# A two-layer attention and expert kernel: layer 0's projections in the order q, k, relative positions of two lines each, V, with a bank of its own for V

## What is computed

```python
qkv = x @ w_qkv + b_qkv                          # q, k, v: (12 heads, 256, 16)
rel_h = jnp.einsum('bhwc,hkc->bhwk', qr, Rh)     # qr = q as (12, 16, 16, 16)
rel_w = jnp.einsum('bhwc,wkc->bhwk', qr, Rw)
attn = jnp.einsum('bmd,bnd->bmn', q, k) * scale
attn = attn + rel_h[:, :, :, :, None] + rel_w[:, :, :, None, :]
p = jax.nn.softmax(attn, axis=-1)
o = jnp.einsum('bmn,bnd->bmd', p, v)
return o @ w_o + b_o
```

## Time and profile before

| | us |
|---|---|
| median of 3 runs | 238.82 |
| lowest, highest | 236.95, 240.77 |
| the profiled execution | 235.63 |
| its span, first to last instruction | 233.6 |
| TensorE busy in it | 216.7 |
| mean granted TensorE clock | 0.957 of full |

### The profile page before, as it was taken

The page is one execution under the profiler, slowest core; times in us unless marked ns, Lnnn a source line. Parts: engine busy times, 40 slices in busy tenths (PEclk is TensorE's granted clock), DMA queues, the critical chain, the costliest instruction groups (busy, mean ns, idle before and its releaser), DMA issues.

```text
span 233.6 us, 4218 instructions
## 1 busy us (share of the span) xinstructions
PE 216.7 (93%) x1580; PEld 195.1 (84%) x1580; DVE 103.6 (44%) x334; ACT 68.5 (29%) x197; POOL 37.0 (16%) x60
## 2 busy tenths in 40 slices
PE   7999989869999999999999989799869999999992
PEld 7799877549898999999999789575558999999991
DVE  2340687568623122222222234886569564723221
ACT  2031087525221212222222131666522021211100
POOL 5220300011990000000000014000014950000000
PEclk9996799997999999999999999958999999999997
DMA  6999999936000000000000000999900000500001
GB/s 169 349 425 423 438 454 424 440 140 153 0 3 0 3 0 0 3 1 0 3 0 0 3 6 15 369 425 426 385 6 1 0 0 15 191 0 3 0 3 41
DMA packets 4492, 31.05 MB, mean 133 GB/s; under 512 B 584, under 2 KB 2064, under 8 KB 2192
## 3 DMA queue, kind: packets, MB, share of 16 engines
q1 hardware_dynamic: 4464, 30.69, 33.6%
HBM read 30.50 MB, written 0.20 MB: 131 GB/s over the span
## 4 chain that ended last, share of the span: by engine, by line
PE 90%; ACT 4%; issue 2%; DVE 2%; POOL 0%; DVEq 0%; ACTq 0%; POOLq 0%
PE bank L1150 17%; PE bank L1137 13%; PE bank L916 9%; PE bank L1135 8%; PE bank L1139 7%; PE bank L985 6%; PE bank L1158 5%; PE bank L940 5%; PE bank L1036 4%; PE bank L970 4%; PE bank L997 3%; PE bank L1122 3%; PE bank L1167 1%; ACT scratch L517 1%; DVE neg_max L661 1%
## 5 line engine op out<-in xcount | busy, mean ns | idle before, releaser
L1150 PE MATMUL bank<-w,scratch 128*96 128x192 f32 (+2 forms) x228 | 52.0, 330 | 0.1
L1137 PE MATMUL bank<-xe_lo,w 128*128 128x192 f32 (+3 forms) x168 | 43.3, 339 | 0.0
L750 DVE TENSOR_TENSOR scratch<-scratch,bank 128x96 f32<-128x96 f32 (+5 forms) x60 | 15.2, 253 | 52.8 <-ACT scratch L475 52.8
L1150 PEld LDWEIGHTS bank<-w,scratch 128*96 128x96 f32 (+2 forms) x228 | 30.7, 164 | 1.5 <-issue 0.3
L475 ACT ACTIVATE scratch<-bank 128x96 f32<-128x96 f32 (+5 forms) x60 | 15.0, 249 | 55.3 <-PE bank L1139 55.3
L1135 PE MATMUL bank<-scratch,w 128*128 128x96 f32 (+3 forms) x168 | 30.8, 265 | 0.0
L1135 PEld LDWEIGHTS bank<-scratch,w 128*128 128x128 f32 (+3 forms) x168 | 27.7, 185 | 3.0 <-issue 3.0
L1139 PE MATMUL bank<-scratch,w 128*128 128x96 f32 (+3 forms) x168 | 29.9, 259 | 0.0
L1139 PEld LDWEIGHTS bank<-scratch,w 128*128 128x128 f32 (+3 forms) x168 | 29.0, 185 | 0.4
L517 ACT ACTIVATE scratch<-bank,neg_max 128x256 f32<-128x256 f32 x48 | 19.8, 477 | 18.9 <-DVE neg_max L661 18.9
L1137 PEld LDWEIGHTS bank<-xe_lo,w 128*128 128x128 f32 (+3 forms) x168 | 24.9, 187 | 0.0
(11 more groups left out here) (160 smaller groups left out, 254.4 us busy)
## 6 DMA issues: line engine op xcount, KB each, us to landing
w<-experts_dram SPq DMA_DIRECT2D x9, 1152.0 KB, 12.3
w<-experts_dram SPq DMA_DIRECT2D x1, 3624.0 KB, 41.8
w<-experts_dram SPq DMA_DIRECT2D x1, 3024.0 KB, 33.7
w<-experts_dram SPq DMA_DIRECT2D x1, 2496.0 KB, 26.6
w<-experts_dram SPq DMA_DIRECT2D x1, 2016.0 KB, 21.2
w<-experts_dram SPq DMA_DIRECT2D x1, 1704.0 KB, 16.9
w<-experts_dram SPq DMA_DIRECT2D x1, 1416.0 KB, 12.2
w<-experts_dram SPq DMA_DIRECT2D x1, 1272.0 KB, 9.3
```

Of the source, the lines that this page charges most:

```text
L750: nc.vector.tensor_tensor(hidden[0:m, n % RING, 0], silu_g[0:m, n % 2, :], up_bank(n)[0:m, 1], ALU.mult).then_inc(sems["hidden_vec"], 1)
L1137: nc.tensor.matmul(tile.rearrange("p u s -> p (u s)"), w0[:, begin + short:begin + short + m], lo.rearrange("p u s -> p (u s)"), start=Fal ...
L1150: ins = nc.tensor.matmul(y_bank(e)[0:SLOTS, 0:C], hidden[0:m, n % RING, u], w0[0:m, begin + at:begin + at + C], start=t == 0 and u == 0, s ...
```

## The change

In layer 0 the order becomes q, k, relative positions, V; in layer 1 it stays k, q, V. V goes to bank 6 in both layers. Each relative-position product takes two lines (96 columns); the second line's result is wrong for that window, and the next product writes over it. The last line of an axis is taken alone. `rel_psum` counts up after each half of an axis, so ScalarE and VectorE start on a half as soon as it is there, and VectorE goes by halves first and groups second. V waits for ScalarE's copies of the first axis, which read bank 6. V's bias is added after the maximum of head 2, in both layers, and the wait for it moves from the first turn to the first weighing. The products on `ones` before the scores of layer 0 go from 10 to 2, and 4 more (`KEEP_FIRST`) are put between the second pair of scores and the first turn, in both layers. q's weights are loaded ahead of k's, and `rel_t` ahead of V's and the parameters. The routing is the same in both kernels.

```diff
-KEEP_START, KEEP_SCORES, KEEP_ROUTE, KEEP_PLACE, KEEP_NORM = 12, (10, 7), 6, 5, 16
+KEEP_START, KEEP_SCORES, KEEP_FIRST, KEEP_ROUTE, KEEP_PLACE, KEEP_NORM = 12, (2, 7), 4, 6, 5, 16
...
+            sp.dma_start(att[0:CH, :, W_Q:W_K], weights[0][:, :, W_Q:W_K]).then_inc(q_landed, 16)
             sp.dma_start(att[0:CH, :, W_K:W_V], weights[0][:, :, W_K:W_V]).then_inc(k_landed, 16)
-            sp.dma_start(att[0:CH, :, W_Q:W_K], weights[0][:, :, W_Q:W_K]).then_inc(q_landed, 16)
+            sp.dma_start(rel_t[:], rel_in).then_inc(rel_landed, 16)
             sp.dma_start(att[0:CH, :, W_V:W_END], weights[0][:, :, W_V:W_END]).then_inc(rest_landed, 16)
             sp.dma_start(par[:], params).then_inc(par_landed, 16)
-            sp.dma_start(rel_t[:], rel_in).then_inc(rel_landed, 16)
...
-                            pool.wait_ge(rel_ready, 2 * (g + 1))
+                            pool.wait_ge(rel_ready, HG + g + 1)
...
-                    act.wait_ge(rel_psum, 1)
                     for half in range(2):
+                        act.wait_ge(rel_psum, half + 1)
...
+                def add_v():
+                    dve.wait_ge(v_psum, layer + 1)
+                    dve.wait_ge(par_landed, 16)
+                    for t in range(TT):
+                        nc.vector.tensor_tensor(v1[:, t, :, 0:HD], bank[6][:, t * C:(t + 1) * C].rearrange("p (h d) -> p h d", d=HD),
+                                                par[:, layer, B_V:B_V + C].rearrange("p (h d) -> p h d", d=HD), ALU.add).then_inc(v_ready, 1)
...
-                    dve.wait_ge(rel_psum, 2)
                     dve.wait_ge(rel_half, 2)
-                    for g in range(HG):
-                        for half, b in enumerate((7, 3)):
+                    for half, b in enumerate((7, 3)):
+                        dve.wait_ge(rel_psum, 3 + half)
+                        for g in range(HG):
...
-                        dve.wait_ge(rel_ready, 2 * (g + 1))
-                        nc.vector.tensor_copy(rel_hi[:, g], relT[:, g]).then_inc(rel_rounded, 1)
+                            if half == 1:
+                                dve.wait_ge(rel_ready, HG + g + 1)
+                                nc.vector.tensor_copy(rel_hi[:, g], relT[:, g]).then_inc(rel_rounded, 1)
...
+                    if h == 2:
+                        add_v()
...
+                if g == 0:
+                    pe.wait_ge(v_ready, TT * (layer + 1))
...
+                    project_q()
+                    pe.wait_ge(k_landed, 16)
+                    project_k()
...
-                            last = nc.tensor.matmul(bank[banks[i // 8]][:, at:at + HG * GRID], window, lines[:, i],
+                            wide = 1 if i + 1 == GRID else 2
+                            last = nc.tensor.matmul(bank[banks[i // 8]][:, at:at + wide * HG * GRID], window, lines[:, i:i + wide],
                                                     start=True, stop=True)
-                        last.then_inc(rel_psum, 1)
+                            if i % 8 == 7:
+                                last.then_inc(rel_psum, 1)
+                    pe.wait_ge(rest_landed, 16)
+                    pe.wait_ge(rel_half, 2)
+                else:
+                    project_k()
+                    project_q()
+                for t in range(TT):
+                    last = project_tokens(bank[6][:, t * C:(t + 1) * C], t, slice(W_V, W_V + C))
+                last.then_inc(v_psum, 1)
...
                 scores(layer, 1)
-                pe.wait_ge(v_ready, TT * (layer + 1))
+                keep_clock(KEEP_FIRST, 5)
```

More of the change, by code:

```diff
@@ L640, in attend @@
                                                    ALU.mult, ALU.add).then_inc(q_split, 1)
-                    if g == 0:
-                        dve.wait_ge(v_psum, layer + 1)
-                        dve.wait_ge(par_landed, 16)
-                        for t in range(TT):
-                            nc.vector.tensor_tensor(v1[:, t, :, 0:HD], bank[4][:, t * C:(t + 1) * C].rearrange("p (h d) -> p h d", d=HD),
-                                                    par[:, layer, B_V:B_V + C].rearrange("p (h d) -> p h d", d=HD), ALU.add).then_inc(v_ready, 1)
                 if layer == 0:
-                    dve.wait_ge(rel_psum, 2)
                     dve.wait_ge(rel_half, 2)
-                    for g in range(HG):
-                        for half, b in enumerate((7, 3)):
+                    for half, b in enumerate((7, 3)):
+                        dve.wait_ge(rel_psum, 3 + half)
+                        for g in range(HG):
                             cols = relT[:, g, :].rearrange("p (r c) -> p c r", c=GRID)[:, 8 * half:8 * half + 8]
@@ L1003, in attend, with project_k, project_q @@
             def attend(layer):
-                if layer == 0:
-                    pe.wait_ge(k_landed, 16)
-                else:
+                if layer == 1:
                     pe.wait_ge(att_landed, 16)
-                for g in range(HG):
-                    last = project(bank[g // 2][:, (g % 2) * TOK:(g % 2 + 1) * TOK],
-                                   W_K + g * P)
-                last.then_inc(k_psum, 1)
+                def project_k():
+                    for g in range(HG):
+                        last = project(bank[g // 2][:, (g % 2) * TOK:(g % 2 + 1) * TOK], W_K + g * P)
+                    last.then_inc(k_psum, 1)
+                def project_q():
+                    for g in range(HG):
+                        last = project(bank[2 + g // 2][:, (g % 2) * TOK:(g % 2 + 1) * TOK], W_Q + g * P)
+                    last.then_inc(q_psum, 1)
                 if layer == 0:
                     pe.wait_ge(q_landed, 16)
-                for g in range(HG):
-                    last = project(bank[2 + g // 2][:, (g % 2) * TOK:(g % 2 + 1) * TOK], W_Q + g * P)
-                last.then_inc(q_psum, 1)
-                if layer == 0:
-                    pe.wait_ge(rest_landed, 16)
-                for t in range(TT):
-                    last = project_tokens(bank[4][:, t * C:(t + 1) * C], t, slice(W_V, W_V + C))
-                last.then_inc(v_psum, 1)
-                if layer == 0:
+                    project_q()
+                    pe.wait_ge(k_landed, 16)
+                    project_k()
                     pe.wait_ge(rel_landed, 32)
```

## The result

| | us |
|---|---|
| changed kernel, median of 4 runs (lowest, highest) | 230.44 (228.84, 231.82) |
| kernel before, median of its 4 runs beside them | 239.45 (236.95, 240.77) |
| ratio, with its 95% interval | 0.9655 (0.9544 to 0.9766) |
| profiled execution: time, span | 230.48, 228.4 |
| mean granted clock in it | 0.982 (before 0.957) |

The change makes the kernel faster by 3.5% by the ratio, and by 3.8% by the two medians.

What follows compares the result with a forecast made beforehand. TensorE's chain, 90% of the span, was taken to bound the kernel. From the profiled 235.63 us, - 5.3 (front) + 0.3 (V's addition) - 1.2 (products before the first turn) gave 229.4, plus 3.2 to the median: 232.6 us, range 229.0 to 237.0.

Steps and rivals of the forecast that it cites:

- rival B: Layer-0 front, second-axis products: strided reads stretch 96-column passes up to 0.224 us, costing 3.6 us, so 236.2 us; chance 0.14.
- the filler: Four products on `ones` before the first turn, both layers: avoid a clock fall in layer 1, 1.2 us gained.
- Order of the projections: Layer-0 front: with q projected first, the relative-position products start at 12.57 instead of 14.18 us; 1.6 us gained.
- Two lines, the clock: Layer-0 relative-position products: 96 columns instead of 48 keep the clock from falling; 2.0 us gained together with the pace.
- Two lines, the pace: Layer-0 relative-position products: all 64 wide passes start 0.112 us apart, 7.2 us in all, ending at 19.7 us.
- Behind the products: Layer-0 front, last product to first score: V's 8 passes and 4 on `ones`, first score at 21.7; 1.7 us gained.
- V's addition: VectorE's queue, both layers, between third maximum and copy of head 0: delays the copy; 0.3 us lost in all.
- Four products before the first turn: Hole after the last score, both layers: avoid layer 1's clock fall, 0 to 2.4 us gained, 1.2 taken.
- The 3.2 us between profile and median: Whole kernel: the median lay 3.2 us above the profiled 235.63 us; added to 229.4 to give 232.6 us.
- Rival D: Layer 0's attention runs at half clock: 8.7 us lost against 2.0 gained, 245.5 us, slower; chance 0.03.

## Why the prediction was right, and where it was not

It said 232.6 us (229 to 237) and faster; 230.4 was measured, inside. By its own signs, though, it was wrong in the front: it was to be wrong if the first score stood later than 23 us, and that stands at 23.24; and rival B's sign, passes of the second axis over 0.112 apart at clock 1.00, was seen. With the front as measured and all else as stated, the sum would have given 234.2. That the time came out under the forecast is owed to the filler and to the median, which were worth more than the sum had for them; in this the number was lucky. Step by step:

- **Order of the projections.** Products at 12.57 foreseen, 12.58 measured; the undoing gives the 1.6 us back. Right.
- **Two lines, the clock.** Right for the front, and shown both ways: without it the clock falls in the changed kernel, and with it alone it stays in the one before. The rule of the Trainium skill's "TensorE: Matmul & The Clock Gate" ("Why this matters for your kernels"), by which only idle gaps count, would have been wrong: TensorE was busy 3.80 of 3.80 us before the fall at 16.7.
- **Two lines, the pace.** Wrong by 1.6 us: 64 x 0.112 did not hold for the 30 wide passes of the second axis (0.165). The step that failed is the one that set rival B aside: I took the 14 ns by which a 48-column pass was longer as all that the stepped read cost, and doubled it, on 80 ns of columns for which no row stands. But a cost under the weight load's 0.112 does not show in the pace, and the bound that the row gives (0.224) stood in the text. The truth lay half way. The Trainium skill ("SBUF — State Buffer", the note on SBUF "cachelines") had the direction right. The run with q in line order agrees with it (0.11 for 0.165); whether it is the crossing of 16-byte lines that costs, no run here tells.
- **Behind the products.** Foreseen 2.0 us from the last product's start plus one step (19.7) to the first score (21.7); measured 2.0 (21.25 to 23.24). Both paths meet there, as stated. Right.
- **V's addition.** 0.15 and 0.2 us foreseen, 0.3 in all. Measured from the first turn to the copy: 0.72 (26.07 to 26.79) for 0.66 in layer 0 and 0.71 for 0.67 in layer 1 (the row of its first turn before is below): 0.1 in all. Against the third maximum's end, the sign that I had named, the copy is not late at all: 0.45 behind it for 0.48, and 0.44 for 0.44. I had started the addition at the end of the third maximum; it starts 0.08 before that end.

The rows of layer 1, for the earlier trace rows, the first one from the kernel before and the others from the changed one:

```profile
150.09 1.34 PE L985 MATMUL bank<-const,scratch 128*128 128x128 f32 x8 [1.67 <-issue]
...
144.52 1.16 PE L920 MATMUL bank<-ones 128*128 128x128 f32 x8
...
146.21 1.39 PE L989 MATMUL bank<-const,scratch 128*128 128x128 f32 x8 [0.53 <-ACT scratch L517]
146.39 0.61 DVE L639 TENSOR_TENSOR v<-bank,par 128x192 f32<-128x192 f32 x2
146.92 0.68 DVE L675 COPY scratch<-bank 128x512 f32<-128x512 f32 x1
```

- **Four products before the first turn.** Direction right, size wrong. I gave them 0 to 2.4 us and took 1.2. By the medians the kernel before gains 4.5 us by them alone, and the changed kernel loses 5.3 to 6.4 without them. My bound was one fall of 6.8 us in one execution. In the attentions the falls last 6.8 to 17 us, and hit layer 0's as well as layer 1's.
- **The 3.2 us between profile and median** were carried over as if they were fixed. They were half-clock stretches that the profiled execution happened to lack, as the second trace of the kernel before shows for one of the longer executions (3.45 us), and the change removes most of them: the changed kernel's profiled execution and median are 230.48 and 230.44.

So the sum is made of errors that offset each other in part: 1.6 us of gain too much in the front, 0.2 too little at the addition, and so some 3.6 too little at the filler and at the median (232.6 + 1.6 - 0.2 = 234.0, and 230.4 was measured). The forecast of 229.4 for the profiled execution (230.48) was good for the same reason: layer 1's attention gave 2.0 and not 1.2, its routing took 1.4 back, which I had not foreseen, and 0.7 more came behind it, in layer 1's experts and at the end. Rival D's limit does not fit its own sum either: 8.7 us lost gave 245.5 us, well over 2%, while it says that it decides from 10. No run came near it.

The parts do not add: width alone -5.9, filler alone -4.5, the order 2.9 to 4.1 by its undoing, together -8.3 to -9.0. The width and the filler each keep the clock up somewhere, and a stretch that is at full clock in one execution can't be gained again by another part.

**Open.** Why the same hole in layer 1 brings the clock down in one trace of the kernel before and leaves it up in its second trace and in the kernel before with two lines. When the hole comes may be the reason, but no run moved a hole by itself. The trade seen in the traces (fronts that gained time lost it in the routing) is of the same kind and is shown as a fact only. Not undone by themselves are V's place behind the products and its own bank, the finer counts of `rel_psum`, and the order of the loads; what they are worth is read from the timeline alone.

## What to carry to other kernels

Read the granted clock of several executions before you price anything from one trace: here the profiled one was among the shortest, and the ordinary one that was traced took 3.45 us more, with 6.8 us more at half clock, against the 5.15 that the two first traces lie apart. Where TensorE stands for a microsecond or two (1.1 to 1.7 us here), try products on a constant, and see whether gains upstream still arrive at the end; here 1.67 us gained in the front were gone by the end of layer 0's routing, and 0.8 of them arrived once the routing was filled. A cost that lies under a weight load can't be read from the pace; before columns are doubled, take what the pace allows as its upper bound, and keep the moving operand in sequence.

## What the runs showed of the hardware

- A full queue did not keep the clock: with 48-column fp32 passes every 0.112 us, TensorE busy all the time (3.80 of 3.80 and 4.89 of 4.92 us), it fell to 1.2 GHz at 16.7 and 19.07 us. With 96 columns in the same passes it stayed at 2.4 until the first score in all nine traces of such a front.
- fp32 columns read with a step of 64 bytes cost 1.7 ns each per pass (0.165 us for 96); in sequence, 96 columns go at the same 0.112 us as 48, under the loading of 128 weight columns.
- A fall lasted 3.4, 6.8, 10.2 or 17.0 us in these traces, and in the attention and routing stretches shown TensorE was busy nearly all the time (3.40 of 3.40 us, 6.78 of 6.80, 17.00 of 17.00), so its busy share showed nothing of it.
- Where the falls come differs between executions of one program: two traces of the kernel before had them in layer 1's attention and in layer 0's, and two of the changed kernel were at half for 3.4 and 6.8 us in layer 1's routing (230.48 and 232.86 us).
- Some executions ran at a mean clock of 0.55 (348 us). They occurred in several of the kernels, the one before among them (354.69 us at 0.552), and no part of the change explains them.
